# Flamingo block on Trainium2: rows of token scales from a transpose of a repeated column instead of a product of ones with a diagonal matrix

## The chip, the cores and the metric

The kernel runs on one core of one Trainium2 chip. The metric is device time in microseconds for one execution of the whole program. The core has five engines that run at the same time and meet by semaphores: PE (TensorE: matmuls and transposes into PSUM), DVE (VectorE), ACT (ScalarE), POOL (GpSimd) and SP (SyncE, which here issues DMAs).

## What is computed

Sixteen batches of 128 tokens with 512 features go through gated cross attention and then through a gated feed-forward layer whose matmuls quantise their inputs per token:

```python
def act_quant(x):
    scale = 127.0 / jnp.clip(jnp.max(jnp.abs(x), axis=-1, keepdims=True), EPS)
    q = jnp.clip(jnp.round(x * scale), -128.0, 127.0) / scale
    return x + jax.lax.stop_gradient(q - x)
...
def h_bitlinear(x, w):
    xq = act_quant(fwht(x))          # Hadamard transform, then 8 bits per token
    wq = weight_quant(w)             # ternary
    return jnp.einsum('bsh,oh->bso', xq, wq)
...
gate = h_bitlinear(hidden_states, w_gate)
up = h_bitlinear(hidden_states, w_up)
return h_bitlinear(jax.nn.silu(gate) * up, w_down)
...
x = x + jnp.tanh(g_xattn[0]) * xattn(_layernorm(x), ctx_512, ctx_512)   # 32 query heads, 8 key heads of 16
x = x + jnp.tanh(g_ffn[0]) * ffn(_layernorm(x), w_gate, w_up, w_down)
```

The scale of a token (its largest absolute value over 127, times the scale of the weights) is needed twice for the first two products: once for the gate, in a row along the free dimension, since the outputs have tokens along that dimension, and once for the up product.

## The kernel before

**Stages.** The program is one stream of instructions per engine, written by hand; the order in each stream is the order of the code, and semaphores (named in `sem("...")`) tie the streams together. First come 16 attention steps, one for each batch. Then the feed-forward layer runs in four units of four batches (`UB = 4`, 512 tokens; a batch within a unit is called a block here, `tb` 0 to 3). For a unit the stages are: `gate_up` (integer inputs times ternary weights, L879; DVE multiplies the gate with the row of scales, L1473, ACT takes silu, L1173, DVE forms the hidden values, L1478), `transform` (the Hadamard transform of the hidden values: products with `had_f`, L933, a split into two parts by ACT, L1203, and DVE, L1453, and products with `had16_r`, L945 and L947), and `project` (L956). `transform` runs as well while the inputs of the next unit are prepared in it, which happens three times: for units 1, 2 and 3. The inputs of unit 0 are prepared inside the attention stage, one block in two steps.

**Inputs of a block in the transform.** `apply` on ACT (L1167) normalises the batch, `front` on POOL (L550 to L557) does two steps of the Hadamard transform, PE turns the result (`first_turn`, L815), ACT copies it (L1156), PE multiplies with `had_f` into bank 1 (`first_had`, L822; it waits for `f_qf`, that is, until the block before has left the bank). DVE then runs `input_peak`: largest absolute value (L1421), two small steps (L1424, L1426), the two scales for gate and up into columns 4 and 5 of `f_max` (L1427), and the scaling that leaves the bank (L1430, gives `f_qf`). Some steps later it runs `input_round`: integers in bf16 into `q_b` (L1439), then `diag` (L1440: the identity times the gate's scale, a diagonal matrix with the scales of the 128 tokens) and `m8u` (L1441: the same for the up scale, in eight columns), both giving `f_dg`. SP sends `q_b` through a transposing DMA (L313, gives `q1_in`), for which `gate_up` waits at its start. PE's `second_turn` waits for `f_dg` and multiplies a matrix of ones with `diag` (L832), which puts the scale of token c into column c of every row, and `gm` with `m8u` (L833), and gives `f_t2`; ACT copies the rows into `s_row` (L1160, gives `f_sg`).

**Where it is in the order.** In step s of `transform`, PE does the products L933 of s, then L945 and L947 of s - 2, then the input work due in that step: turns in steps 0, 3, 6, 9, products with `had_f` in 2, 5, 8, 11, second turns in 6, 9, 12, 15. DVE does L1453 of s, then peaks in steps 3, 6, 9, 12 and rounds in 4, 7, 10, 13. Nothing is reordered by a scheduler.

**In the attention stage** the same is done for unit 0: `early_peak` and `early_round` on DVE (L1358 to L1369), `early_scales` on POOL (`diag`, L489, and `m8_first`, L490), and `early_second` on PE (L758), followed by ACT's copy L1132.

## Time and profile before

| | us |
|---|---|
| median of 3 runs | 470.04 |
| lowest and highest | 469.97, 470.77 |
| profiled execution, its own time | 473.62 |
| its span | 471.8 |

| engine | busy us | share | instructions |
|---|---|---|---|
| PE matmul | 455.3 | 96% | 3108 |
| PE weight load | 292.4 | 62% | 3128 |
| DVE | 386.3 | 82% | 715 |
| ACT | 293.1 | 62% | 522 |
| POOL | 216.6 | 46% | 335 |

The profiled execution is longer than the runs without a profile; changes in us are read from it and taken off the median. Matmuls overlap one another, so that the duration of one is more than the time by which it holds up the next; the distance from start to start tells that time. The chain of waits is followed back from the last instruction, and gives the pieces of time that set the end. "issue" in it is time in which the engine waited for nothing that the profile shows. In the chain of waits PE has 70% of the span, DVE 10%, POOL 7%. The attention stage ends at about 175 us; the three transforms with inputs in them begin at 207, 281 and 356 us.

### The profile page before, as it was taken

Reading aid. Unit: us, or ns where it says so; the run is one execution under the profiler, and the core shown is the slowest. Engines: PE = TensorE matmul, PEld = TensorE weight load, DVE = VectorE, ACT = ScalarE, POOL = GpSimd, SP = SyncE. Lnnn points to the kernel's source line nnn. Section 1 sums busy time; section 2 is a strip of 40 time slices with the busy share of each in tenths; the row PEclk is TensorE's granted clock in tenths of the full one; section 3 lists DMA queues with packets and bytes.
Section 4 is the critical chain, followed back from the end, with each engine's and each line's share of the span. In section 5 each row is a group of like instructions: output and inputs, shape, how many; then the busy total and the mean of one; then the engine's idle time right before and its main releaser. Section 6 shows DMA issues by size and latency. Waiting matters only on the chain.

```text
span 471.8 us, 9054 instructions
## 1 busy us (share of the span) xinstructions
PE 455.3 (96%) x3108; PEld 292.4 (62%) x3128; DVE 386.3 (82%) x715; ACT 293.1 (62%) x522; POOL 216.6 (46%) x335
## 2 busy tenths in 40 slices
PE   9999999999999989989999999999999999999997
PEld 8755555555555534468944479864468874479664
DVE  5778998787877749868998967999885999889891
ACT  3378897677777788777647417643616663647460
POOL 4235646889898454655005734202926300930000
PEclk9799999999999999999999999999999999999999
DMA  8999020121013241000200651100361110153086
GB/s 240 328 348 350 18 57 13 24 58 24 13 24 102 23 123 78 2 0 14 24 11 1 111 135 33 22 12 0 67 156 46 24 24 0 29 92 60 1 139 218
DMA packets 68183, 35.90 MB, mean 76 GB/s; under 512 B 50288, under 2 KB 62960, under 8 KB 68144
## 3 DMA queue, kind: packets, MB, share of 16 engines
q1 hardware_dynamic: 67408, 34.48, 29.0%
q10 hardware_dynamic: 736, 0.92, 0.7%
q8 instruction: 22, 0.36, 0.4%
q14 instruction: 17, 0.14, 0.1%
HBM read 19.26 MB, written 4.19 MB: 50 GB/s over the span
## 4 chain that ended last, share of the span: by engine, by line
PE 70%; DVE 10%; POOL 7%; issue 6%; ACT 4%; DMA 2%; ACTq 0%; DVEq 0%; POOLq 0%
PE ps L879 16%; PE ps L956 11%; PE ps L933 9%; PE ps L608 7%; PE ps L630 4%; PE ps L673 4%; PE ps L690 3%; PE ps L945 2%; PE ps L947 2%; PE ps L822 2%; PE ps L638 2%; DMA x_all<-in_x 2%; DVE y_split L1453 2%; DVE mz L1492 1%; PE ps L732 1%
## 5 line engine op out<-in xcount | busy, mean ns | idle before, releaser
L879 PE MATMUL ps<-wst 128*128 128x512 bf16 x499 | 111.7, 380 | 3.2 <-DVE wst L1473 2.0
L1310 DVE TENSOR_REDUCE reg<-ps 128x4 f32<-128x512 f32 x128 | 81.7, 683 | 25.6 <-PE ps L630 24.0
L879 PEld LDWEIGHTS ps<-wst 128*128 128x128 bf16 x512 | 49.1, 98 | 62.1 <-DVE wst L1473 3.9
L572 POOL TENSOR_TENSOR reg_rest<-reg_rest,z_sc 128x1024 f32<-128x1024 f32 x24 | 47.3, 2008 | 84.6 <-DVE z_sc L1515 84.6
L1037 ACT ACTIVATE reg<-ps 128x512 f32<-128x512 f32 x116 | 62.9, 596 | 26.5 <-PE ps L638 25.4
L630 PE MATMUL ps<-reg 32*128 32x256 f32 x512 | 74.2, 405 | 0.7 <-DVE reg L1310 0.7
L1173 ACT ACTIVATE wst<-wst 128x512 f32<-128x512 f32 x64 | 40.0, 626 | 51.3 <-DVE wst L1473 51.0
L608 PE MATMUL ps<-reg 32*128 32x512 f32 x232 | 70.1, 639 | 0.0
L933 PE MATMUL ps<-had_f,wst 128*128 128x128 f32 x512 | 67.1, 276 | 1.1 <-DVE wst L1478 1.1
L933 PEld LDWEIGHTS ps<-had_f,wst 128*128 128x128 f32 x512 | 64.0, 192 | 4.3 <-DVE wst L1478 1.8
L1203 ACT CAST y_split<-ps 128x512 fp32r<-128x512 f32 x64 | 37.3, 584 | 36.3 <-PE ps L933 36.3
L1453 DVE TENSOR_TENSOR y_split<-ps,y_split 128x512 fp32r<-128x512 f32 x64 | 43.5, 683 | 14.5 <-ACT y_split L1203 14.5
L1473 DVE TENSOR_TENSOR wst<-ps,wst 128x512 f32<-128x512 f32 x64 | 43.5, 680 | 8.3 <-PE ps L879 8.2
L630 PEld LDWEIGHTS ps<-reg 32*128 32x128 f32 x512 | 47.0, 186 | 2.9 <-ACT reg L1064 1.1
L1478 DVE TENSOR_TENSOR wst<-ps,wst 128x512 f32<-128x512 f32 x64 | 43.4, 678 | 1.4 <-ACT wst L1173 1.3
L956 PE MATMUL ps<-wst,reg_rest 128*128 128x512 bf16 x186 | 42.2, 380 | 0.4
L1212 ACT COPY reg_rest<-ps 128x512 f32<-128x512 f32 x64 | 37.9, 592 | 2.2 <-PE ps L947 2.1
L1492 DVE TENSOR_REDUCE mz<-reg_rest 128x8 f32<-128x1024 f32 (+1 forms) x33 | 38.3, 1171 | 0.0
L463 POOL TENSOR_TENSOR x_all<-x_all,reg 128x256 f32<-128x256 f32 x32 | 24.1, 753 | 26.7 <-DVE reg L1323 26.6
L956 PEld LDWEIGHTS ps<-wst,reg_rest 128*128 128x128 bf16 x192 | 27.4, 145 | 13.9 <-issue 0.6
L608 PEld LDWEIGHTS ps<-reg 32*128 32x128 f32 x232 | 21.5, 183 | 21.1 <-ACT reg L1037 10.2
L673 PE MATMUL ps<-reg 128*32 128x512 f32 x256 | 34.1, 605 | 0.1
(173 smaller groups left out, 766.1 us busy)
## 6 DMA issues: line engine op xcount, KB each, us to landing
wst<-in_w SPq DMA_DIRECT2D x16, 512.0 KB, 8.0
reg<-in_w SPq DMA_DIRECT2D x8, 512.0 KB, 5.7
out<-x_all SPq DMA_DIRECT2D x16, 256.0 KB, 2.1
x_all<-in_x SPq DMA_DIRECT2D x3, 1024.0 KB, 9.2
reg<-in_v SPq DMA_DIRECT2D x4, 256.0 KB, 3.6
reg<-in_k_t SPq DMA_DIRECT2D x28, 32.0 KB, 2.7
x_all<-in_x ACTq DMA_DIRECT2D x1, 512.0 KB, 7.6
reg_rest<-reg SPq DMA_TRANSPOSE x20, 3.0
```

The costliest lines, as they stand in the source:

```text
L572: pool.tensor_tensor(z, z, sc, ALU.mult).then_inc(sem("z_scaled"), 1)
L608: pe.matmul(ps[:, column_bank(c, m), :], kpad[b // CHUNK % 2][strip(i), b % CHUNK, a, :], q_t[b % 4][strip(i), :], start=True, stop=False)
L630: last = pe.matmul(ps[:, row_bank(r, m), 256 * g:256 * g + 256], q_t[n % 4][strip(i), P * h:P * h + P], kpad[n // CHUNK % 2][strip(i), n % ...
L673: last = pe.matmul(O_BANK[SLOT * l:SLOT * l + SLOT, :], v_pad[n // CHUNK % 2][:, n % CHUNK, 4 * kvh + l, :], probs[:, 4 * kvh + l, :], sta ...
L879: last = pe.matmul(ps[:, banks[ob % n], :], tern_gu[:, ob // 2, m, j, P * (ob % 2):P * (ob % 2) + P], q1_t[:, j, :], start=(j == 0), stop= ...
L933: last = pe.matmul(ps[:, Y_BANKS[s % 3], P * k:P * k + P], X[:, 4 * s + k, :, :].rearrange("p c t -> p (c t)"), had_f[:, :], start=True, s ...
L956: last = pe.matmul(ps[:, bank, :], q2.rearrange("p g (t c) -> p c (g t)", c=NC)[:, c, P * tb:P * tb + P], tern_d[:, c, :], start=(c == 0), ...
L1037: act.activation(probs[:, 2 * j + m, :], ps[:, column_bank(c, m), :], ACT.Exp, scale=D ** -0.5).then_inc(sem("exp_done"), 1)
L1310: dve.tensor_reduce(neg_max[n % 2][:, g:g + 2, i + m, :], ps[:, row_bank(r, m), :].rearrange("p (g a t) -> p g a t", g=2, a=2), AX_X, ALU. ...
L1453: dve.tensor_tensor(y_low[s % RING], ps[:, Y_BANKS[s % 3], :], y_high[s % RING].bitcast(F32), ALU.subtract).then_inc(sem("y_low"), 1)
L1473: dve.tensor_tensor(gs[ob % GS], ps[:, G_BANKS[ob % 2], :], s_row, ALU.mult).then_inc(sem("gs_done"), 1)
L1478: dve.tensor_tensor(X[:, :, ob, :], ps[:, U_BANKS[ob % 3], :].rearrange("p (g t) -> p g t", g=NG), gs[ob % GS].rearrange("p (g t) -> p g t ...
```

## The change

The scales of a block go to columns 4 and 5 of `f_max` for even blocks and to columns 6 and 7 for odd ones (`scales_at`). `diag` is no longer written for the scales, neither on DVE (L1440) nor on POOL (L489). PE reads the column of the gate's scales as if it were a 128x128 matrix whose columns are all that column (`broadcast_to`), and transposes it; the result has the scale of token c in column c of every row, as before. `f_dg` now counts one for each block, not two. `early_second` waits for `f_c` (the scales are written) in place of `f_dg`. Since PE now reads `f_max` itself, DVE has a new wait before it writes a pair of scales: for `f_t2` of two blocks earlier (and in the attention stage for `f_dg` too).

```diff
+        def scales_at(tb):
+
+            return 4 + 2 * (tb % 2)
+
+        def scale_rows(tb):
+
+            return f_max[:, scales_at(tb):scales_at(tb) + 1].broadcast_to([P, P])
...
                 pool.wait_ge(sem("f_c"), 4 * tb + 4)
-                reach(pool, sem("f_t2"), tb)
-                pool.tensor_scalar(diag[:, :], ident_f[:, :], f_max[:, 4:5], None, ALU.mult).then_inc(sem("f_dg"), 1)
-                pool.tensor_scalar(m8_first[:, tb, :], t8m[:, :], f_max[:, 5:6], None, ALU.mult).then_inc(sem("f_dg"), 1)
+                up = scales_at(tb) + 1
+                pool.tensor_scalar(m8_first[:, tb, :], t8m[:, :], f_max[:, up:up + 1], None, ALU.mult).then_inc(sem("f_dg"), 1)
...
-                pe.wait_ge(sem("f_dg"), 2 * tb + 2)
+                pe.wait_ge(sem("f_c"), 4 * tb + 4)
                 pe.wait_ge(sem("fin_done"), 2 * b - 1)
-                pe.matmul(T_BANK[:, 256:256 + P], ones_f[:, :], diag[:, :], start=True, stop=True).then_inc(sem("f_t2"), 1)
+                pe.transpose(T_BANK[:, 256:256 + P], scale_rows(tb), ident_f[:, :]).then_inc(sem("f_t2"), 1)
...
-                reach(pe, sem("f_dg"), n.times(2, 2))
+                reach(pe, sem("f_dg"), n.times(1, 1))
...
-                pe.matmul(ps[:, 2, 256:256 + P], ones_f[:, :], diag[:, :], start=True, stop=True)
+                pe.transpose(ps[:, 2, 256:256 + P], scale_rows(tb), ident_f[:, :])
...
-                dve.tensor_scalar(f_max[:, 4:6], wsc[:, 0:2], f_max[:, 1:2], C_E, ALU.mult, ALU.mult
+                if tb > 1:
+                    dve.wait_ge(sem("f_t2"), tb - 1)
+                    dve.wait_ge(sem("f_dg"), tb - 1)
+                at = scales_at(tb)
+                dve.tensor_scalar(f_max[:, at:at + 2], wsc[:, 0:2], f_max[:, 1:2], C_E, ALU.mult, ALU.mult
...
-                dve.tensor_scalar(f_max[:, 4:6], wsc[:, 0:2], f_max[:, 1:2], C_E, ALU.mult, ALU.mult
+                reach(dve, sem("f_t2"), n.times(1, -1))
+                at = scales_at(n.const)
+                dve.tensor_scalar(f_max[:, at:at + 2], wsc[:, 0:2], f_max[:, 1:2], C_E, ALU.mult, ALU.mult
...
-                dve.tensor_scalar(diag[:, :], ident_f[:, :], f_max[:, 4:5], None, ALU.mult).then_inc(sem("f_dg"), 1)
-                dve.tensor_scalar(m8u[:, :], t8m[:, :], f_max[:, 5:6], None, ALU.mult).then_inc(sem("f_dg"), 1)
+                up = scales_at(tb) + 1
+                dve.tensor_scalar(m8u[:, :], t8m[:, :], f_max[:, up:up + 1], None, ALU.mult).then_inc(sem("f_dg"), 1)
```

Line numbers of the changed kernel are 7 to 13 higher than those of before. On DVE, in the transform, from the reciprocal of block 0's peak to the write of `m8u`, the stream of before is this (`wst` holds the scaled values, `few` the weights' scales):

```order
L1426 RECIPROCAL f_max<-f_max 128x1 [waits f_c]
L1427 TENSOR_SCALAR f_max<-few,f_max 128x2
L1429 REGISTER_ALU
L1430 TENSOR_SCALAR wst<-ps,f_max 128x512 [waits f_c]
L61 REGISTER_ALU
L1453 TENSOR_TENSOR y_split<-ps,y_split 128x512 [waits y_out]
L61 REGISTER_ALU [waits f_qf]
L61 REGISTER_ALU [waits f_t2]
L1439 TENSOR_SCALAR q_b<-wst 128x512 [waits q1_in3]
L1440 TENSOR_SCALAR diag<-ident_f,f_max 128x128
L1441 TENSOR_SCALAR m8u<-t8m,f_max 128x8
```

and in the changed kernel, with the lines of the changed code:

```order
L1437 RECIPROCAL f_max<-f_max 128x1 [waits f_c]
L61 REGISTER_ALU
L1440 TENSOR_SCALAR f_max<-few,f_max 128x2 [waits f_t2]
L1442 REGISTER_ALU
L1443 TENSOR_SCALAR wst<-ps,f_max 128x512 [waits f_c]
L61 REGISTER_ALU
L1466 TENSOR_TENSOR y_split<-ps,y_split 128x512 [waits y_out]
L61 REGISTER_ALU [waits f_qf]
L61 REGISTER_ALU [waits f_t2]
L1452 TENSOR_SCALAR q_b<-wst 128x512 [waits q1_in3]
L1454 TENSOR_SCALAR m8u<-t8m,f_max 128x8
```

One 128x128 write is gone from between `q_b` and `m8u`, and the write of the two scales has a wait, with one register instruction ahead of it. On PE, in step 6 of the transform, the second turn of block 0 stands between the products with `had16_r` and the turn of block 2; before:

```order
L945 MATMUL ps<-y_split,had_r 128x512 [waits z_out,y_low]
L947 MATMUL ps<-y_split,had_r 128x512
L832 MATMUL ps<-diag,ones_f 128x128 [waits f_su,f_sg,f_dg]
L833 MATMUL ps<-m8u,gm 64x8
L61 REGISTER_ALU
L815 MATMUL ps<-ident_f,scratch4k 128x128 [waits f_xt,f_b2]
```

and after:

```order
L952 MATMUL ps<-y_split,had_r 128x512 [waits z_out,y_low]
L954 MATMUL ps<-y_split,had_r 128x512
L839 MATMUL ps<-ident_f,f_max 128x128 [waits f_su,f_sg,f_dg]
L840 MATMUL ps<-m8u,gm 64x8
L61 REGISTER_ALU
L822 MATMUL ps<-ident_f,scratch4k 128x128 [waits f_xt,f_b2]
```

The order and the waits are the same; the instruction in third place is another one.

## Rows read from the trace of the kernel before

**Rows 1.** The page: busy time of the engines, and the granted clock in 40 slices.
```profile
PE 455.3 (96%) x3108; PEld 292.4 (62%) x3128; DVE 386.3 (82%) x715; ACT 293.1 (62%) x522; POOL 216.6 (46%) x335
...
PEclk9799999999999999999999999999999999999999
```

**Rows 2.** Chain of waits, first transform: start us, us, engine, tile, line.
```profile
208.19 0.44 PE ps L815 x4
...
216.94 0.77 DVE diag L1440
217.71 0.63 DVE m8u L1441
...
222.82 0.14 issue
222.96 1.13 PE ps L822 x8
...
225.44 0.22 PE ps L832 x2
```

**Rows 3.** Groups by form: line, engine, tiles, shapes, count | busy us, mean ns | idle.
```profile
L815 PE MATMUL ps<-ident_f,scratch4k 128*128 128x128 f32 x48 | 7.8, 286 | 0.2
...
L832 PE MATMUL ps<-diag,ones_f 128*128 128x128 f32 x24 | 4.6, 273 | 0.0
...
L489 POOL TENSOR_SCALAR diag<-ident_f,f_max 128x128 f32<-128x128 f32 x4 | 2.6, 661 | 0.0
```

**Rows 4.** Timeline, first transform, ACT, POOL and DVE: start us, us, instruction, idle before.
```profile
214.91 0.21 DVE L1427 TENSOR_SCALAR f_max<-few,f_max 128x2 f32<-128x2 f32 x1
...
216.17 0.59 ACT L1203 CAST y_split<-ps 128x512 fp32r<-128x512 f32 x1
...
216.89 0.73 POOL L556 TENSOR_TENSOR scratch4k<-wst 128x256 f32<-128x256 f32 x1 [0.16 <-POOL wst L551]
...
217.58 0.73 POOL L557 TENSOR_TENSOR scratch4k<-wst 128x256 f32<-128x256 f32 x1
...
221.27 0.72 POOL L550 TENSOR_TENSOR wst<-wst 128x256 f32<-128x256 f32 x1 [2.97 <-ACT wst L1167]
...
221.55 0.47 DVE L1427 TENSOR_SCALAR f_max<-few,f_max 128x2 f32<-128x2 f32 x1
...
229.65 0.28 DVE L1440 TENSOR_SCALAR diag<-ident_f,f_max 128x128 f32<-128x128 f32 x1
...
229.85 0.23 DVE L1441 TENSOR_SCALAR m8u<-t8m,f_max 128x8 f32<-128x8 f32 x1
```

**Rows 5.** Attention stage: chain of waits, and (third row) POOL's timeline.
```profile
115.52 0.42 PE ps L758 x2
...
174.25 0.18 ACT wst L1132
...
120.03 0.23 POOL L476 TENSOR_SCALAR ve<-mv 128x1 f32<-128x1 f32 x1 [0.16 <-DVE mv L1272]
```

**Rows 6.** Timeline, first transform, PE around the products of blocks 1 and 2.
```profile
216.20 0.40 PE L947 MATMUL ps<-y_split,had_r 128*128 128x512 f32 x1
216.44 1.05 PE L822 MATMUL ps<-had_f,wst 128*128 128x128 f32 x8
...
222.17 0.39 PE L947 MATMUL ps<-y_split,had_r 128*128 128x512 f32 x1
```

**Rows 7.** Timeline, end of the first transform, all engines; last row: tile `q_b`.
```profile
231.01 0.59 ACT L1203 CAST y_split<-ps 128x512 fp32r<-128x512 f32 x1 [1.20 <-PE ps L933]
...
231.71 0.68 DVE L1453 TENSOR_TENSOR y_split<-ps,y_split 128x512 fp32r<-128x512 f32 x1
...
235.24 1.19 SPq L313 DMA_TRANSPOSE wst<-q_b  x1
...
237.77 2.29 PEld L879 LDWEIGHTS ps<-wst 128*128 128x128 bf16 x12 [0.40 <-issue]
...
DMA to landing us min/median/max: 2.4/2.4/4.3
```

More of the change, by code:

```diff
@@ L755, in early_second @@
                 tb = EARLY_SECOND[b]
-                pe.wait_ge(sem("f_dg"), 2 * tb + 2)
+                pe.wait_ge(sem("f_c"), 4 * tb + 4)
                 pe.wait_ge(sem("fin_done"), 2 * b - 1)
-                pe.matmul(T_BANK[:, 256:256 + P], ones_f[:, :], diag[:, :], start=True, stop=True).then_inc(sem("f_t2"), 1)
+                pe.transpose(T_BANK[:, 256:256 + P], scale_rows(tb), ident_f[:, :]).then_inc(sem("f_t2"), 1)
             def early_groups():
-                pe.wait_ge(sem("f_dg"), 2 * UB)
+                pe.wait_ge(sem("f_dg"), UB)
                 for tb in range(UB):
```

## The prediction

> **What bounds the kernel now.** I read the page's first two parts, then the chain of waits of one transform stage (205 to 240 us), then the timeline of that stretch engine by engine, then the chain of the attention stage. The first tells that PE is busy 96% of the span and that its clock is granted at nine tenths or more in all slices but one [rows 1]: whatever takes no time off PE, or off a wait of PE, is worth nothing. Durations and granted clock leave little to gain from the clock. The edit acts in two places: the attention stage, where it is done four times (tb 0 to 3 of the first unit), and the transform, which runs three times with four blocks each (12 in all). I work out the first transform; in the other two the chain shows the same wait before L822, 0.14 us behind L1430 as in [rows 2].
>
> In the transform the chain lies on DVE up to 222.82 us, and in it stand, one behind the other, the removed write of `diag` (0.77 us) and the write of `m8u` (0.63 us). DVE then releases the third block's product with `had_f` on PE (L822, 222.96), and from there to the end the chain stays on PE, with the product of ones and `diag` in it three times at 0.22 us [rows 2]. So there are two terms: DVE time before 222.8 us, and PE time behind it.
>
> **PE's part.** The product is fp32 and goes in two passes: 24 instructions for 12 products, while a transpose goes in one, 48 for 48 blocks [rows 3]. In the chain four transposes step on at 0.44 us, 0.11 each, and the two passes at 0.22 [rows 2]. I take 0.11 us off each product. The new operand is one column of `f_max` read 128 times; no row shows such a read, so its price is bounded from the rows: 0.11 us as for a full block, up to the 0.42 us that the dearest row for this product shows (in the attention stage, behind L673 [rows 5]); I take 0.11, the row of the same kind of instruction. A transpose of L815 lasts 286 ns by its row, but overlaps its neighbours; were all of that on the path, it would be 0.07 us dearer than the old product, rival (b) below. The Trainium skill (TensorE: Matmul & The Clock Gate, Part 4: PE-mode transpose) speaks against the edit in the same way: it puts a transpose at about 275 ns inside a kernel, and taken as time on the path that would lead to the sum of (b).
>
> **DVE's part.** Each of the 12 blocks loses one write of 128x128. Free, it takes 0.28 us, and L1441 starts 0.20 behind it; but in the first block of a transform it starts at 216.94, 0.05 us after POOL's L556, and ends at 217.71, 0.09 after that one does; and then L1441 ends at 218.34, 0.03 us after POOL's next, L557 [rows 2, 4]. Two small writes wait for one POOL instruction each. Without the first, L1441 stands where L1440 stood, ends with L556 at about 217.7 and not at 218.34: 0.63 us less, the length of the L1441 piece in the chain [rows 2]. The second wait goes and the first stays. The next DVE step (L1453) does not hold it up: its input from ACT is there at 216.76 [rows 4]. A second gain may come with it: L1427 of block 1 takes 0.47 us, started 0.28 us into POOL's L550, and 0.21 where POOL is idle [rows 4]; moved up by 0.6 us it lies ahead of L550, for another 0.26. What is late next is then PE itself.
>
> Against it stands the new wait on `f_t2` between the reciprocal and L1427. It asks for the second turn of the block before the last, which is long past (block 3's needs block 1's, which PE runs at 225.44, and comes behind 231.71 [rows 2, 7]), so only its own handling costs, and behind it are queued L1430 and the rest of DVE. Bounds: nothing, if the register arithmetic hides under the reciprocal, and 0.14 us, the gap from a DVE end to the instruction that it releases [rows 2]; I take 0.05, since the semaphore is met and no event has to travel. Two of them lie before L822: 0.1 us. DVE gives 0.63 - 0.10 = 0.53, with the second gain 0.79.
>
> How much of that PE can take: its L947 before the wait starts at 222.17; without a wait L822 follows L947 by 0.24 us (216.20 to 216.44), here it follows by 0.79 [rows 6]. PE's idle time is 0.55 us, and with block 0's 0.11 off PE can be ready 0.66 earlier. So L822 moves up by 0.53 to 0.66 us.
>
> **The end of the transform.** What starts the next stage? L879 starts loading weights at 237.77. The transposing DMA of block 3 was issued at 235.24 and lands 2.4 us later, at 237.64, 0.13 us before [rows 7]. It is the landing that is late, not PE; in the other two transforms the same sum gives 0.16 and 0.13. So what counts is when DVE writes `q_b` of block 3. That write goes back, without a gap on DVE, to L1453 at 231.71, whose input from ACT was ready at 231.60 [rows 7] and comes from PE. PE is there earlier by 0.53 to 0.66 and block 1's 0.11, so 0.64 to 0.77; with the 0.11 of slack DVE can gain up to 0.88, and it loses 0.05 in block 3's own new wait. The gain of a transform is 0.59 to 0.83 us. Block 2's and block 3's 0.11 on PE are hidden: the first falls behind the step that feeds 231.71, the second lies beside PE's wait for the last L1453. I take 0.75, since the cheap L1427 is likely: 3 x 0.75 = 2.25 us. The writes of `diag` in blocks 1 and 2 keep DVE ahead of PE and give nothing more.
>
> **The attention stage.** The product stands in the chain three times at 0.42 us (115.52, 136.40 and 156.10 us), each with 0.11 to lose: 0.33 us [rows 5]. The fourth does not count: there ACT's copy (L1132) ends the wait, behind ACT work [rows 5]. POOL loses four writes of `diag`, 0.66 us each [rows 3], but none is on the path: behind the first, POOL catches up and then waits 0.16 us for DVE [rows 5], and it is the DVE statistics that start the chain that POOL holds up to PE's next turn. If that cover were gone they would bring up to 0.6 us. PE now waits for `f_c` where it waited for `f_dg`, an earlier event. The tests of `f_t2` and `f_dg` before L1363 are met two batches earlier.
>
> **Sum:** 2.25 + 0.33 = 2.6 us. The profiled execution took 473.62 us (span 471.8); it would take 471.0. It lies 3.6 us above the median of the runs; I take the difference off the median: 470.04 - 2.6 = 467.4.
>
> **Rivals.** (a) *The wait for POOL is handed on.* If L1441 is not let in behind L556 but still ends with L557 at 218.34, DVE gains nothing and loses 0.1 to the new waits; PE's 0.11 of block 1 pays that back, and 0.33 of the attention stage stays: 469.7. For it speaks that POOL starts L557 before L1440 has ended; against it, that L1440, queued just so, did get in between the two [rows 2, 4]. The Trainium skill (SBUF — State Buffer, SBUF: two separate sides) calls the pair of ports that DVE and GpSimd share an exclusive lock that whichever starts first holds for the whole instruction. By that rule, which this trace's 0.77 against 0.28 us bears out, both outcomes are open.
>
> (b) *A transpose costs its whole duration, 0.29 us, on the path.* Then PE is 0.07 later, not 0.11 earlier, at each place. DVE still gives 0.53; PE can take 0.48, and block 1 costs 0.07: 0.4 a transform, 1.2 in all, less 0.21 in attention: 469.0. Against it stand the 0.11 steps of L815 [rows 2].
>
> (c) *Slower: reading one column 128 times is slow.* The mechanism sits in the weight load before each transpose. With x us for the transpose instead of 0.22, about twelve of them count (three in attention, three in each transform), and the idle 0.55 is there to be filled: 3 x 0.55 - 12 (x - 0.22). That is zero at x = 0.36, and slower by over 0.2% from x = 0.44 on. At 0.56 us it is -2.4: 472.4. Nothing in the trace speaks for it.
>
> (d) *More.* The DVE side becomes free of POOL in block 1 as well, POOL's relief is felt in attention, and the cap of 0.88 is reached without a cost of the wait: 3 x 0.9 + 0.44 + 0.3 = 3.4: 466.6.
>
> **How the numbers follow.** Forecast (2.0 to 3.0 us off) 0.62; (a) 0.13; (b) 0.10; (c) 0.05; (d) 0.10. 0.2% is about 0.94 us, what a measurement of this kernel can tell from no change. Faster: forecast, (d) and about half of (b), 0.78; same: (a) and the rest of (b), 0.17; slower: 0.05. The range goes from (d), 466.6, to between (b) and (a), 469.3; outside stay (c), most of (a) and a little of (d).
>
> **What would show it.** In the profile after: PE instructions fewer by 16 and one pass per transpose; L822 of block 2 right behind L947 with a gap of 0.24 or little more; the write of `m8u` in block 0 ending with the first of POOL's two second-step instructions; q_b of block 3 to L879 still 2.4 us and some tenths. (a) shows as `m8u` of block 0 still ending with the second POOL instruction. (b) and (c) show as the step from the new transpose to the next PE instruction, above 0.2 or above 0.4 us. I would be wrong altogether if the start of L879 turns out to hang on something else than the landing, or if the stage behind gives the time back.

## The result, and the profile after it

| | us |
|---|---|
| before, median (lowest to highest) | 470.0 (469.84 to 470.77) |
| after, median of 4 runs (lowest to highest) | 466.57 (466.49 to 466.68) |
| ratio after to before, 95% interval | 0.992, 0.9896 to 0.9943 |
| after, profiled execution, its own time | 466.68 |
| its span | 464.8 |

The change gains 3.4 us. The forecast was 2.6 us and 467.4, with a range that began at 466.6; the direction and the place were right, the size was not. A second set of runs of the same kernel gave 466.73, 3.2 us under before and just inside that range. Single executions of several kernels, before among them, are up to 2% longer at a mean granted clock of 0.985 to 0.993, where the others have 0.999 or 1.0; they hardly move the medians.

The page after, where it answers to [rows 1]: PE has 16 instructions fewer by the matmuls' weight loads (3128 to 3112), and the clock is granted at nine tenths in all slices.

```profile
PE 450.1 (97%) x3112; PEld 285.9 (61%) x3112; DVE 382.1 (82%) x703; ACT 293.5 (63%) x522; POOL 214.6 (46%) x331
...
PEclk9999999999999999999999999999999999999999
...
PE 74%; POOL 8%; issue 6%; DVE 6%; ACT 4%; DMA 1%; POOLq 0%; DVEq 0%; ACTq 0%
```

The profiled execution of before lies 3.6 us above its median, and its stages show where: the first stretch, up to the first transpose of L741 (L748 in the changed kernel), takes 3.7 us more than in the changed kernel (89.79 against 86.07 us), at a lower clock in one slice [rows 1]. So the two traces are compared stage by stage behind it. A stage is measured here from the first weight load of PE in it to the first of the next; weight loads have all their records in these traces, matmuls lack some.

| stage, us | before | after | difference |
|---|---|---|---|
| attention, from L741 to the first transform | 117.24 | 116.81 | -0.43 |
| first transform / gate_up behind it | 30.74 / 29.57 | 29.83 / 29.51 | -0.91 / -0.06 |
| second | 31.05 / 29.54 | 30.09 / 29.54 | -0.96 / 0.00 |
| third | 30.74 / 29.56 | 29.78 / 29.87 | -0.96 / +0.31 |
| from the last product with `had16_r` to the end | 30.25 | 30.02 | -0.23 |

A transform and the gate_up behind it belong together, since what the one gains at its end the other can give back: 60.31, 60.59 and 60.30 us before, 59.34, 59.63 and 59.65 after. That is 0.97, 0.96 and 0.65 us, 2.58 in all, and with attention 3.0 us. The last row, which starts with the first weight load of L956 behind that product, is not touched by the edit. It takes 30.25 to 30.36 us in the five kernels that have the product of two passes anywhere, before among them, and 30.01 to 30.20 in the traces of all others, with 30.02 and 30.20 for the changed kernel itself. So it may be a side effect of the change; no run isolates it, and its cause is open.

Lines of the changed kernel are 7 higher than before on PE and ACT (L822, the product with `had_f` for the inputs, is L829 now; L832 is L839; L879 is L886), and 11 to 13 higher on DVE (L1427 is L1440, L1439 is L1452, L1441 is L1454, L1453 is L1466, L1473 is L1486, L1492 is L1505).

The chain of waits of the first transform, from the first block's second turn on, against [rows 2] (start us, us, engine, tile, line):

```profile
214.71 0.11 PE ps L839
214.82 0.21 PE ps L840 x2
...
218.09 0.23 PE ps L954
218.32 0.89 PE ps L829 x8
...
220.57 0.11 PE ps L839
```

Before, DVE's writes of `diag` (0.77) and `m8u` (0.63) stood in it, then 0.14 us of issue and L822 with 1.13 us. After, the chain stays on PE from 209 us to the end of the transform. L829 starts behind L954 without a gap and takes 0.89 us there. The new transpose takes 0.11 us in the chain, the old product took 0.22.

The timeline of POOL and DVE at block 0, against [rows 4] (start us, us, engine, instruction, idle time before it):

```profile
212.58 0.42 DVE L1452 TENSOR_SCALAR q_b<-wst 128x512 bf16<-128x512 f32 x1
212.75 0.83 POOL L563 TENSOR_TENSOR scratch4k<-wst 128x256 f32<-128x256 f32 x1 [0.16 <-POOL wst L558]
212.91 0.70 DVE L1454 TENSOR_SCALAR m8u<-t8m,f_max 128x8 f32<-128x8 f32 x1
213.52 0.68 DVE L1466 TENSOR_TENSOR y_split<-ps,y_split 128x512 fp32r<-128x512 f32 x1
213.53 0.73 POOL L564 TENSOR_TENSOR scratch4k<-wst 128x256 f32<-128x256 f32 x1
```

The write of `m8u` (0.22 us when alone) now takes the place that `diag` had: it starts during POOL's first second-step instruction, ends 0.03 us behind it (213.61 against 213.58), and DVE goes on before the next one counts. One wait of two is gone. Rival (a), the wait handed on to POOL's next instruction, is refuted by these rows. The Trainium skill (SBUF — State Buffer, SBUF: two separate sides) has an exclusive lock on the shared ports, held for a whole instruction. The trace agrees that `m8u` ends only behind the POOL instruction that started first, 0.70 against 0.22 us; which of the two engines comes next, the section does not say, and here it is DVE, ahead of POOL's second instruction.

In the attention stage the piece of the chain is 0.25 us where [rows 5] has 0.42, three times (first row of three):

```profile
111.84 0.25 PE ps L765
```

### The profile page after: what moved, and what is told of

Its sections match the earlier page's. It is cut to its first block, busy times and chain, and to the rows that moved or that the text cites. A ratio compares the mean times of both kernels' runs of the same rounds, so it can differ in the third digit from the quotient of the medians.

```text
span 464.8 us, 9025 instructions
## 1 busy us (share of the span) xinstructions
PE 450.1 (97%) x3112; PEld 285.9 (61%) x3112; DVE 382.1 (82%) x703; ACT 293.5 (63%) x522; POOL 214.6 (46%) x331
## 4 chain that ended last, share of the span: by engine, by line
PE 74%; POOL 8%; issue 6%; DVE 6%; ACT 4%; DMA 1%; POOLq 0%; DVEq 0%; ACTq 0%
PE ps L886 16%; PE ps L963 12%; PE ps L940 11%; PE ps L615 7%; PE ps L637 5%; PE ps L680 5%; PE ps L952 3%; PE ps L954 3%; PE ps L697 3%; PE ps L829 2%; PE ps L645 2%; PE ps L822 1%; PE ps L739 1%; DVE wst L1491 1%; DVE wst L1486 1%
## 5 line engine op out<-in xcount | busy, mean ns | idle before, releaser
L886 PE MATMUL ps<-wst 128*128 128x512 bf16 x512 | 113.1, 379 | 2.3 <-DVE wst L1486 2.0
L886 PEld LDWEIGHTS ps<-wst 128*128 128x128 bf16 x512 | 49.2, 98 | 62.3 <-DVE wst L1486 4.0
L637 PE MATMUL ps<-reg 32*128 32x256 f32 x512 | 72.6, 400 | 0.3 <-ACT reg L1071 0.2
L1466 DVE TENSOR_TENSOR y_split<-ps,y_split 128x512 fp32r<-128x512 f32 x64 | 43.5, 684 | 15.7 <-ACT y_split L1210 15.7
L1486 DVE TENSOR_TENSOR wst<-ps,wst 128x512 f32<-128x512 f32 x64 | 43.7, 682 | 8.3 <-PE ps L886 8.3
L637 PEld LDWEIGHTS ps<-reg 32*128 32x128 f32 x512 | 46.0, 184 | 2.2 <-ACT reg L1071 0.7
L1505 DVE TENSOR_REDUCE mz<-reg_rest 128x8 f32<-128x1024 f32 (+1 forms) x33 | 38.3, 1174 | 0.2 <-issue 0.2
L615 PEld LDWEIGHTS ps<-reg 32*128 32x128 f32 x232 | 21.5, 183 | 21.1 <-ACT reg L1044 10.2
```

The source lines that it names most:

```text
L615: pe.matmul(ps[:, column_bank(c, m), :], kpad[b // CHUNK % 2][strip(i), b % CHUNK, a, :], q_t[b % 4][strip(i), :], start=True, stop=False)
L637: last = pe.matmul(ps[:, row_bank(r, m), 256 * g:256 * g + 256], q_t[n % 4][strip(i), P * h:P * h + P], kpad[n // CHUNK % 2][strip(i), n % ...
L886: last = pe.matmul(ps[:, banks[ob % n], :], tern_gu[:, ob // 2, m, j, P * (ob % 2):P * (ob % 2) + P], q1_t[:, j, :], start=(j == 0), stop= ...
L1466: dve.tensor_tensor(y_low[s % RING], ps[:, Y_BANKS[s % 3], :], y_high[s % RING].bitcast(F32), ALU.subtract).then_inc(sem("y_low"), 1)
L1486: dve.tensor_tensor(gs[ob % GS], ps[:, G_BANKS[ob % 2], :], s_row, ALU.mult).then_inc(sem("gs_done"), 1)
```

## The experiments

Each is an edit of the changed kernel, beside which it is read. One table has all medians and, from the traces, the time of attention and of each transform with its gate_up; the texts below refer to it. The experiments were run in four sets, the first of them the changed kernel's second, each with "before" in it, whose median lay between 469.82 and 469.98. Differences of stages are taken from the changed kernel's first trace.

| kernel | median us | attention | transform with gate_up, three |
|---|---|---|---|
| changed kernel, first set | 466.57 | 116.81 | 59.34, 59.63, 59.65 |
| changed kernel, second set | 466.73 | 116.83 | 59.37, 59.65, 59.65 |
| two passes everywhere | 468.14 | 117.29 | 59.67, 59.94, 59.99 |
| two passes in attention | 467.19 | 117.20 | 59.36, 59.60, 59.63 |
| two passes in block 2 | 467.36 | | 59.48, 59.71, 59.76 |
| two passes in block 3 | 467.03 | | 59.34, 59.60, 59.66 |
| write of `diag` in all blocks | 468.56 | 116.86 | 60.11, 60.36, 60.11 |
| in block 0 | 467.92 | 116.86 | 59.97, 60.26, 59.99 |
| in blocks 1 to 3 | 467.68 | 116.85 | 59.80, 60.04, 59.77 |
| write of `diag` on POOL | 466.59 | 116.85 | 59.36, 59.61, 59.64 |
| four pairs, no new waits | 466.48 | 116.87 | 59.34, 59.60, 59.33 |
| `q_b` early | 467.01 | | 59.51, 59.77, 59.82 |
| one reduction later | 472.66 | | 60.81, 61.04, 61.71 |
| one reduction later, `q_b` early | 472.54 | | 62.57, 61.16, 60.59 |
| DVE stream moved by four | 466.21 | | 59.36, 59.61, 59.32 |
| half reductions | 466.06 | | 59.23, 59.47, 59.19 |
| half reductions, `q_b` early | 465.67 | | 59.06, 59.48, 59.04 |

### The changed kernel again

> The changed kernel again, as the base line on the same chip as the three experiments beside it. Both theories expect its 466.6 us, 3.4 us under the kernel before.

466.73 us, 0.16 over the first set, with the same times of attention and of each transform with its gate_up, to 0.03 us. Inside the second of these gate_up starts 0.16 us later than in the first set (30.25 against 30.09) and is shorter by as much. So 0.2 us between medians of different sets says nothing here, nor does 0.16 at that one boundary, and small terms are read from the stages.

### The product's two passes back, on PE alone

```diff
-                pe.transpose(ps[:, 2, 256:256 + P], scale_rows(tb), ident_f[:, :])
+                pe.matmul(ps[:, 2, 256:256 + P], scale_rows(tb), ident_f[:, :], start=True, stop=True)
```
and the same in `early_second`.

> The changed kernel, with a product of the repeated column and the identity in place of each transpose, in the transform and in the attention stage: two passes again on PE, DVE and POOL as in the changed kernel. Theory (the gain of a transform comes from DVE time ahead of its step for block 2, and only that of the attention stage from PE): a transform gives back the 0.11 us of block 1's product, at most 0.2; the attention stage 3 x 0.17 us (the pieces in its chain of waits fell from 0.42 to 0.25). Together +0.8 us, 0.6 to 1.1, so 467.4. Rival (the passes on PE are the whole gain, as PE is busy 97% of the span): +3 us and more, 470.

+1.4 us, more than the 1.1 that the theory allowed, and far from the 3 of the rival. The stages split it: attention +0.48, and +0.33, +0.31, +0.34 in each transform with its gate_up. That is 0.11 us not for one block but for three. The row by form shows what one instruction of either kind lasts, and that the duration is not the cost: 272 ns for both (columns: line, engine, shapes, count | busy us, mean ns | idle); after, then this kernel:

```profile
L839 PE MATMUL ps<-ident_f,f_max 128*128 128x128 f32 x12 | 3.3, 272 | 0.0
L839 PEld LDWEIGHTS ps<-ident_f,f_max 128*128 128x128 f32 x12 | 1.6, 133 | 0.5
```
```profile
L839 PE MATMUL ps<-ident_f,f_max 128*128 128x128 f32 x24 | 4.6, 272 | 0.0
L839 PEld LDWEIGHTS ps<-ident_f,f_max 128*128 128x128 f32 x24 | 4.5, 188 | 1.0
```

The Trainium skill (TensorE: Matmul & The Clock Gate, Part 4: PE-mode transpose) has about 275 ns for a 128x128 transpose inside a kernel, measured in bf16. As a duration this trace has nearly the same in fp32, 272 ns. As time on the path it is 0.11 us, and taking the duration for that gave rival (b), which is refuted. So is (c): the weight load of a column read 128 times takes 133 ns.

### The write of `diag` back, on DVE alone

In `input_round`, ahead of the write of `m8u`; nobody reads it:

```diff
+                dve.tensor_scalar(diag[:, :], ident_f[:, :], f_max[:, up - 1:up], None, ALU.mult)
```

> The changed kernel, with a write of the 128x128 diagonal matrix, which nobody reads, put back on DVE ahead of the small write in each block of the transforms; PE as in the changed kernel. Theory (DVE time at block 0): two small writes wait for POOL again, the write of the eight columns ends with POOL's second instruction, and each transform is 0.6 to 0.8 us longer: +1.8 to +2.4 us, 468.4 to 469.0. Rival (PE's passes): under +0.4.

+1.8 us; +0.77, +0.73 and +0.46 (0.78 against the 59.33 that the third takes without the idle time treated below). Both terms of the forecast are real. The medians of the two experiments, +1.4 and +1.8 us, add up to the 3.2 us that this set shows, but that agreement is in part luck: in the first transform with its gate_up the two give 0.33 + 0.77 = 1.10 us where the whole change gave 0.97. The wait before block 3's product tells the two apart: it is 0.15 us with the transposes and 0.04 with the product of two passes, where PE comes 0.11 later (table further down).

### The write in block 0 alone, and in blocks 1 to 3 alone

The line above under `if tb == 0:`, and under `if tb > 0:`.

> The same, with the write in block 0 of each transform alone (3 writes, not 12). Theory (only block 0's write stands in the path, since there DVE releases PE's step for block 2; the others leave DVE ahead of PE): the same +1.8 to +2.4 us as with all twelve writes. Rival (each write costs its 0.28 us wherever it stands): a quarter of what the twelve cost, +0.5 us.

> The changed kernel with the unread write of the diagonal matrix on DVE in blocks 1, 2 and 3 of each transform, not in block 0. Theory (only block 0's stands in the path): 0 to +0.3 us against the changed kernel. Rival (each write costs where it stands): three quarters of what twelve cost, +1.4 us or more.

Neither is as expected. Block 0 alone costs 0.63 us for each transform with its gate_up, blocks 1 to 3 alone 0.46, all four 0.77. They are two bounds, one behind the other, not two costs that add. The prediction said of the writes in blocks 1 and 2 that they "keep DVE ahead of PE and give nothing more"; that is false. With block 0's write gone, PE is 0.7 us earlier, and block 1's write would be the next to hold it up. The timeline of the kernel with the write in blocks 1 to 3 shows it. Before, block 1's `diag` started 0.94 us behind the start of POOL's first second-step instruction and waited once, for the second. Here it starts 0.12 us behind, and block 1 has both waits for POOL, as block 0 had in [rows 2]:

```profile
218.56 0.79 POOL L563 TENSOR_TENSOR scratch4k<-wst 128x256 f32<-128x256 f32 x1
218.68 0.75 DVE L1455 TENSOR_SCALAR diag<-ident_f,f_max 128x128 f32<-128x128 f32 x1
219.31 0.72 POOL L564 TENSOR_TENSOR scratch4k<-wst 128x256 f32<-128x256 f32 x1
219.35 0.70 DVE L1456 TENSOR_SCALAR m8u<-t8m,f_max 128x8 f32<-128x8 f32 x1
```

and its chain then has DVE releasing block 3's product, where the changed kernel's has PE alone:

```profile
218.68 0.75 DVE diag L1455
219.43 0.62 DVE m8u L1456
...
223.51 0.76 DVE wst L1443
224.28 0.14 issue
224.41 1.13 PE ps L829 x8
```

The following table sets the positions of PE's weight loads in the first transform beside one another, in us from the transform's start.

| PE's place | before | after | two passes | write in 0 to 3 | in 0 | in 1 to 3 |
|---|---|---|---|---|---|---|
| behind block 0's second turn | 12.17 | 12.09 | 12.19 | 12.09 | 12.06 | 12.08 |
| behind block 2's product with `had_f` | 16.78 | 16.07 | 16.16 | 16.70 | 16.68 | 16.07 |
| behind block 1's second turn | 18.77 | 17.95 | 18.15 | 18.58 | 18.56 | 17.95 |
| behind block 3's product with `had_f` | 22.78 | 21.92 | 22.13 | 22.70 | 22.55 | 22.38 |
| behind block 2's second turn | 24.78 | 23.79 | 24.11 | 24.58 | 24.43 | 24.26 |
| last product with `had_f`, s = 15 | 27.36 | 26.38 | 26.70 | 27.16 | 27.01 | 26.84 |
| start of gate_up | 30.74 | 29.83 | 30.02 | 30.66 | 30.44 | 30.34 |
| end of gate_up | 60.31 | 59.34 | 59.67 | 60.11 | 59.97 | 59.80 |

The row to read is that of s = 15. Its differences from the changed kernel (+0.98, +0.32, +0.78, +0.63, +0.46) are those of the last row (+0.97, +0.33, +0.77, +0.63, +0.46), to 0.01 us. The start of gate_up has others. So in these kernels what PE gains up to its last product with `had_f` is what transform and gate_up gain, and the start of gate_up does not decide. What connects that product with gate_up is DVE. In the changed kernel it waits for the split that this product feeds, and then has no idle time into gate_up, up to PE's transpose of the peaks 8.7 us into it:

```profile
231.19 0.69 DVE L1466 TENSOR_TENSOR y_split<-ps,y_split 128x512 fp32r<-128x512 f32 x1 [0.32 <-ACT y_split L1210]
231.92 0.18 DVE L1460 TENSOR_REDUCE su<-ps 64x8 f32<-64x32 f32 x1
232.03 2.33 DVE L1505 TENSOR_REDUCE mz<-reg_rest 128x8 f32<-128x1024 f32 x2
234.28 0.67 DVE L1486 TENSOR_TENSOR wst<-ps,wst 128x512 f32<-128x512 f32 x1
...
240.64 0.67 DVE L1486 TENSOR_TENSOR wst<-ps,wst 128x512 f32<-128x512 f32 x1
```

The table also gives the gain its parts, down the first two columns: 0.08 us from block 0's second turn, 0.63 from the wait before block 2's product, 0.11 from block 1's turn, 0.04 from a small wait before block 3's, 0.13 from block 2's turn.

### The two passes in block 2 alone, and in block 3 alone

```diff
+                if tb == 2:
+                    pe.matmul(ps[:, 2, 256:256 + P], scale_rows(tb), ident_f[:, :], start=True, stop=True)
+                else:
+                    pe.transpose(ps[:, 2, 256:256 + P], scale_rows(tb), ident_f[:, :])
```

and with `tb == 3`.

> The changed kernel with the product of two passes in place of the transpose for block 2 of each transform alone. Prediction: its 0.11 us is hidden behind the step that feeds q_b of block 3, so no change. Theory (PE has no idle time from there to its last product with had_f, which starts what bounds transform and gate_up): +0.11 us in each of three, 59.45 in place of 59.34.

> The same for block 3 alone. Here the product stands behind PE's last product with had_f, beside PE's wait for the last split. Theory and prediction: no change, 59.34. Rival (every two-pass product costs its 0.11 us): 59.45.

Block 2: 59.48, 59.71 and 59.76, +0.14, +0.08 and +0.11. Block 3: 59.34, 59.60 and 59.66, nothing. The prediction had both as hidden; block 2's stands on the path, because PE has no idle time between it and s = 15, and block 3's comes behind s = 15, beside PE's wait for the last split. The medians of these two, 467.36 and 467.03, have no changed kernel in their set to stand against, so the stages carry this verdict. Of the 0.3 to 0.5 us by which 467.03 lies above the changed kernel's two medians, 0.34 stands in its trace behind the last product with `had16_r` (30.36 us), and is not explained.

### `q_b` of block 3 earlier

```diff
-        INPUT_PEAK, INPUT_ROUND = {3: 0, 6: 1, 9: 2, 12: 3}, {4: 0, 7: 1, 10: 2, 13: 3}
+        INPUT_PEAK, INPUT_ROUND = {3: 0, 6: 1, 9: 2, 12: 3}, {4: 0, 7: 1, 10: 2, 12: 3}
```

> The changed kernel with block 3's q_b written in step 12 of the transform, ahead of the split of step 13, not behind it. Both theories: the transposing DMA is issued about 0.5 us earlier, and each transform ends up to 0.43 us earlier, where PE is through (29.83 to about 29.4 us). Theory (what bounds transform and gate_up together is DVE, which has two reductions of 128x1024 to do, L1505, 2.33 us, before it reads the first gate, L1486; the kernel with four pairs ended each of two transforms 0.15 us earlier, and gave 0.12 to 0.15 back in the gate_up behind): gate_up gives back 0.3 us or more, the two together stay at 59.3, and the median is within 0.4 us of the changed kernel. Rival (the landing is the bound, as the prediction had it): 1.0 to 1.3 us faster, 465.4.

The transposing DMA goes out 0.54 us earlier, at 229.63 instead of 230.17 us. Gate_up starts 0.18 earlier in the first (29.65 against 29.83) and 0.16 in the third; in the second it starts 0.16 later (30.25), as in the changed kernel's second set. But transform and gate_up together are 0.14 to 0.17 us longer in all three, and the median is up by 0.3 to 0.4, at 467.01, against the changed kernel in other sets. The reason stands on DVE: the small reduction L1460 between the last split and the first peak comes 0.17 us later from the transform's start (29.22 against 29.05, with 0.19 us of idle time before it), and all DVE work into gate_up with it:

```profile
231.13 0.69 DVE L1466 TENSOR_TENSOR y_split<-ps,y_split 128x512 fp32r<-128x512 f32 x1 [0.21 <-ACT y_split L1210]
232.02 0.18 DVE L1460 TENSOR_REDUCE su<-ps 64x8 f32<-64x32 f32 x1 [0.19 <-ACT wst L1167]
232.13 2.33 DVE L1505 TENSOR_REDUCE mz<-reg_rest 128x8 f32<-128x1024 f32 x2
234.38 0.67 DVE L1486 TENSOR_TENSOR wst<-ps,wst 128x512 f32<-128x512 f32 x1
```

PE, which came earlier, then waits for DVE up to 9.0 us into gate_up, where the changed kernel's first gate_up has no wait:

```profile
241.47 4.00 PEld L886 LDWEIGHTS ps<-wst 128*128 128x128 bf16 x20 [0.47 <-DVE wst L1486]
```

The landing does bear on the start of gate_up, as the prediction said. The start does not set the end.

### Less work on DVE behind the last split

The two reductions between the last split and the first gate read half of their input, 64 columns of each of the eight groups, not 128; the peaks of the other half are left out.

```diff
-                peak(prev, 3)
-                peak(prev, 4)
+                peak_half(prev, 3)
+                peak_half(prev, 4)
...
+                dve.tensor_reduce(mz[:, g0:g0 + 8], Z[:, g0:g0 + 8, 0:P // 2], AX_X, ALU.max,
+                                  apply_absolute_value=True).then_inc(sem("mz_done"), 1)
```

> The changed kernel with the two reductions between the last split and the first gate (L1505 for q = 3 and 4) over half of their input, 128x512 in place of 128x1024; the peaks of the other half are left out. It takes about 1.1 us off DVE behind the last split of a transform. Theory (transform and gate_up together are bound by PE up to its last product with had_f, s = 15, and from there by DVE, which has no idle time up to PE's wait for a gate 8.8 us into gate_up; the landing of q_b bounds nothing): that wait goes, 0.2 to 0.4 us less for each transform with its gate_up, 59.0 to 59.15 in place of 59.34, the median 0.6 to 1.2 us lower. Rival (the landing is the bound, as the prediction had it): 59.34, no change.

> The same, with q_b of block 3 in step 12 as well, which alone made the kernel 0.16 us slower for each transform with its gate_up. Theory: with DVE's load behind the last split halved, the landing is the next bound, and the earlier q_b now gains what PE has behind its last product, up to 0.2 us each on top of the halved reductions: 58.8 to 58.95. Rival (the earlier q_b costs wherever DVE stands): 0.16 us slower again.

59.23, 59.47 and 59.19: 0.11 and 0.16 us less, where 0.2 to 0.4 was expected. The third is 0.46 less than 59.65, and 0.14 less than the 59.33 that it takes without the idle time of DVE treated below; that idle time is still there, and is hidden now. DVE is the bound there, but by little; something close behind it holds next. With `q_b` early as well the first and third lose another 0.17 and 0.15, the second nothing; alone it cost 0.14 to 0.17. In both kernels each gate_up takes 29.40 us, and what differs is its start: 29.83 and 29.66 in the first, 30.07 and 30.08 in the second. So the next bound is the start of gate_up and with it the landing, 0.1 to 0.15 us behind DVE. Both theories of the end of the transform were nearly true, and DVE is the one that decides in the changed kernel.

### One reduction later

```diff
-                    if chain is not None and ob == 4:
+                    if chain is not None and ob == 5:
...
-                peak(prev, 4)
...
-                        if ob < 3:
-                            peak(prev, 5 + ob)
-                        if ob == 5:
+                        if ob < 4:
+                            peak(prev, 4 + ob)
+                        if ob == 6:
                             chain(prev)
```

> The changed kernel with one of the two reductions L1505 moved from ahead of the first gate to behind the fourth (and what follows from the peaks, PE's transpose L921 and DVE's chain of small steps, each one output block later). Theory (DVE bounds the start of gate_up): the first read of the gate, L1486, comes up to 1.1 us earlier, PE's wait of 0.6 us for it goes, and each gate_up behind a transform is 0.3 to 0.6 us shorter: 0.9 to 1.8 us faster in all, 465.3. Rival (the reductions are hidden, or are merely moved to where DVE is as full): within 0.3 us.

> The two together: q_b of block 3 in step 12, and the reduction moved behind the first gates. Theory (the landing bounds the transform, and DVE the start of gate_up; each alone is given back in part, and both together are not): 1.2 us on top of the later reduction alone, 464.2. Rival (the landing bounds nothing any more): as with the later reduction alone.

472.66 and 472.54, 6 us slower than the changed kernel: each gate_up takes 30.97 us or more where it took 29.51. The timeline of PE names the cause, the small steps of DVE's `chain` that I had moved by one output block, while PE's product behind them (L926) kept its place:

```profile
247.56 0.24 PE L926 MATMUL ps<-ident_f,diag 64*128 64x64 f32 x1 [1.44 <-DVE diag L1522]
```

That wait of 1.44 us is what the first two gate_ups lost (1.47 and 1.44); the third lost 2.05, at a granted clock of 0.95 where the others have 1.00. The profiled execution, at 471.67 us, is 5.0 over the changed kernel's, and the three stages make up 4.9 of it; the median lies 1.0 higher. The second kernel was profiled in one of its longest executions (476.32 us, clock 0.989), so its 62.57 is no measure of the edit. The moved chain swamps what the moved reduction does, and these two tell nothing on either theory.

### POOL's writes back in the attention stage; the two passes there alone

```diff
+                pool.tensor_scalar(diag[:, :], ident_f[:, :], f_max[:, up - 1:up], None, ALU.mult)
                 pool.tensor_scalar(m8_first[:, tb, :], t8m[:, :], f_max[:, up:up + 1], None, ALU.mult).then_inc(sem("f_dg"), 1)
```

> The changed kernel with the four writes of the diagonal matrix, which nobody reads, put back on POOL in the attention stage. Theory (POOL's relief is hidden; the gain of 0.43 us there is PE's): within 0.15 us of the changed kernel. Rival (POOL's 0.66 us each come through, in part): +0.4 to +2.6 us.

466.59, attention 116.85: POOL's four writes, 0.66 us each [rows 3], are hidden, as predicted.

> The changed kernel with the product of two passes in place of the transpose in the attention stage alone. Theory (the pieces in the chain fell from 0.42 to 0.25 us, three of them): +0.5 us, 0.3 to 0.6. Rival (0.11 us each, as the prediction had it): +0.33. Rival (PE's time there is hidden): 0.

467.19 beside 466.59 in the same set, +0.6, and +0.39 by the stage, 0.13 a piece (0.16 with two passes everywhere). Another 0.1 to 0.3 stands behind the last product with `had16_r`, 30.30 against 30.02 to 30.20 us. The chain of this kernel has the old 0.42 us again (first row of three):

```profile
111.76 0.42 PE ps L765 x2
```

### What the new waits cost, and the 0.31 us of the third gate_up

```diff
-            return 4 + 2 * (tb % 2)
+            return 4 + 2 * (tb % UB)
...
-                reach(dve, sem("f_t2"), n.times(1, -1))
```

and the two waits of the attention stage out as well, with `f_max` wide enough for four pairs.

> The changed kernel with four pairs of columns for the scales, one for each block of a unit, and without the new waits of DVE on f_t2 and f_dg, which are then not needed. It measures what the new waits cost. Theory (they cost nothing, since the register arithmetic lies beside the reciprocal: L1437 to L1440 is 0.08 us apart, as without the wait): within 0.15 us of the changed kernel. Rival (0.05 us for each of three in a transform, as the prediction had it): 0.45 us faster, more if the 0.38 us of block 0 in the first transform are the wait.

59.34 and 59.60 for the first two: the new waits cost nothing that can be measured, in the transform or (116.87) in attention. Gate_up starts 0.15 us earlier in the first than in the changed kernel (29.68), and gives it back, 29.66 against 29.51. But the third is 59.33, not 59.65. The changed kernel gives 0.3 us back in its third gate_up, and this one does not. DVE has 0.24 us of idle time there, put down to nothing that is waited for; in the first and second there is none, and those two are one loop in the program while the third is code of its own. The changed kernel, DVE:

```profile
378.51 0.18 DVE L1460 TENSOR_REDUCE su<-ps 64x8 f32<-64x32 f32 x1
378.93 2.34 DVE L1505 TENSOR_REDUCE mz<-reg_rest 128x8 f32<-128x1024 f32 x2 [0.24 <-issue]
```

The idle time is there in both sets of the changed kernel and wherever DVE's instructions are the changed kernel's in number and place (two passes, POOL's writes, early `q_b`, later and half reductions), and not with the extra writes on DVE or with four pairs. So I moved the stream:

```diff
+            for i in range(8, 12):
+                dve.memset(f_max[:, i:i + 1], 0.0)
             dve.memset(kpad[0][:, :, :, :], 0.0).then_inc(sem("k_zero"), 1)
```

with `f_max` twelve columns wide, as with four pairs.

> The changed kernel with four writes of one column each, which nobody reads, ahead of everything on DVE: they lie before any work on the path, and move the rest of DVE's instructions back by four places. Theory (DVE's 0.24 us of idle time before L1505 in the third gate_up alone, in every kernel with the changed kernel's DVE instructions and in none with others, hangs on where the instructions lie in DVE's stream, not on what they wait for): the idle time is gone there, the third gate_up takes 29.55 us, not 29.87, and the median is 0.3 us lower, 466.3. Rival (it comes from the time at which the transform ends): as in the changed kernel.

```profile
378.56 0.18 DVE L1462 TENSOR_REDUCE su<-ps 64x8 f32<-64x32 f32 x1
378.67 2.33 DVE L1507 TENSOR_REDUCE mz<-reg_rest 128x8 f32<-128x1024 f32 x2
```

Gone: 59.32, and 466.21 us, 0.9921 of before (0.9908 to 0.9934). Four useless instructions at the head of DVE's stream take 0.33 us off the third gate_up with its transform, and this kernel has the lowest median of those that compute the whole result, though without the changed kernel in its set. The wider `f_max` is not the cause, since the extra writes on DVE end the idle time with `f_max` eight columns wide; nor is the time at which the stage comes, since two passes and early `q_b` shift it and keep the idle time. So the idle time hangs on where the instructions lie in the stream. What in the chip makes it, is open.

## Why the prediction was right and wrong, point by point

**DVE ahead of block 2's product: right.** The wait is gone, `m8u` ends with POOL's first instruction, L1440 of block 1 takes 0.21 us and not 0.47. Forecast 0.53 to 0.66 us for L822 with block 0's 0.11; measured 0.71 (0.08 and 0.63). The idle time before L822 was read as 0.55 from its gap to L947 [rows 6]; but behind idle time the eight products of L822 also take longer up to the next product's start, 0.96 us against 0.89 in the changed kernel, so that the stall weighed 0.63. That is a mis-sized term, 0.08 us.

**Block 1's product on the path: right,** 0.11 us.

**The end of the transform: the step that failed.** The step was: "It is the landing that is late, not PE", and from it "Block 2's and block 3's 0.11 on PE are hidden" and a cap of 0.88. The landing bears on the start of gate_up, but transform and gate_up together hang on PE's s = 15 and the DVE work behind it. So block 2's 0.13 us counts (two passes in block 2: +0.11), block 3's does not, and the cap is none.

The path alone is the smaller part of the miss. At the start of gate_up, the place that the prediction summed for, the gain was 0.91 us in the first transform and 0.96 in the others, not 0.75, and past the cap too. There the steps were right and the sizes low: PE fed the split of s = 12 0.86 us earlier (0.71, 0.11 of block 1, and 0.04 from a small wait before block 3's product that the prediction left out), not 0.64 to 0.77; DVE's slack gave 0.07 more, and the waits cost nothing. With gate_up behind it the gain was 0.97. Of the 0.22 us missed in the first transform 0.16 are sizes and 0.06 the path. I had named the possibility, "if the start of L879 turns out to hang on something else than the landing, or if the stage behind gives the time back", and never asked DVE's timeline across the boundary: before the change too it runs without idle time from the last split into gate_up, and the trace of before had the rows for that.

**New waits: 0.05 us each was too dear;** they cost nothing (four pairs), where the sum had 0.1 us ahead of L822 and 0.05 in block 3.

Together 0.97 us in place of 0.75, three times: +0.66 on the forecast.

**Attention: right in kind, too small.** Forecast 3 x 0.11; the pieces fell by 0.17, the stage by 0.43, 0.14 each. I had taken the step of the transform for a place where the piece was 0.42, not 0.22.

**The writes in blocks 1 and 2 "give nothing more": wrong,** though it didn't change the sum. The gain of the whole is 0.77 us for DVE; with block 0's write alone taken away it would be 0.31 (all four against 1 to 3). A wait that is hidden before becomes the bound once the one ahead of it goes.

**Not foreseen:** the 0.3 us that the third gate_up gives back.

The sum by stages is then 3 x 0.97 + 0.43 - 0.31 = 3.0 us, by the medians 3.2 and 3.4. Of the last 0.2 to 0.4 us, 0.23 stands between the two traces behind the last product with `had16_r`, where all five kernels with a product of two passes are slower than the others; why, is open.

**The rivals.** (a), (b) and (c) are refuted by the trace after. (d), which had chance 0.10 and 3.4 us, gives the number that came out. Two of its reasons held, that DVE is free of POOL in block 1 and that the new waits cost nothing. One did not: POOL's relief gave nothing in attention. That its sum meets the measured 3.4 is in part luck: the transforms gained more than its 0.9 each, and the third gate_up gave 0.31 back.

## What to carry to other kernels

To find what a gain at a stage's end is worth, don't stop at the instruction that starts the next stage: follow the engine that runs without idle time across the boundary, and look for the first wait behind it. Compare two stages as a pair when the second can give back what the first gains; here one row (PE's last product) told the time of both to 0.01 us, while the boundary between them was off by up to 0.14. And when a stall goes, go through the same waits further down with the engines at their new distance: block 1's write was free only as long as block 0's held everything up.

## What the runs showed of the hardware

- One transpose in fp32 of a column read 128 times by a zero step costs PE 0.11 us where it has work ahead, as much as one of a full 128x128 block, and its weight load takes 133 ns; the two passes of the fp32 product cost 0.22.
- A DVE write of 128x8 takes 0.22 us alone and 0.70 when it starts 0.16 us into a POOL instruction of 0.83; it ends 0.03 us behind that one and doesn't wait for POOL's next, which starts 0.08 us before the write ends.
- DVE stood idle for 0.24 us at one place of straight code, in every kernel with the same instructions in DVE's stream ahead of it, and not when four instructions were put in at its head. It cost that stage 0.3 us. A difference of 0.3 us between two kernels can be no more than this.
